# Second batch of a routed-FFN kernel: its ScalarE, VectorE and TensorE work dealt out anew, and a fifth staging place for expert weights

## What is computed

```python
# attention-like mixer, per batch of 512 tokens
sim = einsum(Q, K) / (sqrt(32) * 4)            # 512 x 512, Q and K from ctx
threshold = top_k(sim, 153)[0][:, :, -1:]      # the 153rd largest of each row
A = sigmoid(sim) * (sim >= threshold)
A = (A + swapaxes(A, -1, -2)) * 0.5
x = x + (1 - g) * layernorm(x) + g * A         # g = sigmoid(gamma_raw)
# feed-forward on xn = layernorm(x), 2048 tokens, 8 experts, 2 for each token
shared = silu(xn @ s_gate_w + s_gate_b) * (xn @ s_up_w + s_up_b) @ s_down_w + s_down_b
moe = sum over experts of weight * (silu(xn @ gate) * (xn @ up)) @ down
out = x + moe + shared
```

## Time and profile before

| what | value |
|---|---|
| median of 3 runs | 521.26 us |
| profiled execution, its own time | 522.16 us |
| its span, first to last instruction | 520.3 us |
| TensorE busy | 457.6 us, 88% of the span |
| VectorE busy | 335.3 us, 64% |
| ScalarE busy | 254.1 us, 49% |
| GpSimd busy | 149.0 us, 29% |
| mean granted TensorE clock | 0.946 |
| chain that ended last | TensorE 73%, VectorE 14%, ScalarE 4% |

### The profile page before, as it was taken

One profiled execution on the slowest core, in us unless ns is written; L12 is line 12 of the kernel. 1 busy time (PEld: TensorE's weight loads), 2 busy tenths in 40 slices (PEclk: granted clock), 3 DMA queues, 4 the chain that ended last, 5 costly groups with the idle time before them and its releaser, 6 DMA issues.

```text
span 520.3 us, 9112 instructions
## 1 busy us (share of the span) xinstructions
PE 457.6 (88%) x2619; PEld 257.8 (50%) x2620; DVE 335.3 (64%) x959; ACT 254.1 (49%) x469; POOL 149.0 (29%) x199
## 2 busy tenths in 40 slices
PE   7406775999999999899997999999999999999960
PEld 3204332545454545354444666666666666666630
DVE  4879799799999999737956555555556433333310
ACT  5884546347934792335543455555545333333320
POOL 2010100013001300220042554555545444444431
PEclk9755996999999999999998999999999999999995
DMA  8801520028302800285368888778777545545541
GB/s 277 240 1 69 179 96 2 0 81 195 70 1 82 146 18 1 94 151 110 90 164 213 189 201 190 189 174 199 182 185 171 87 84 85 86 82 88 90 69 22
DMA packets 39005, 60.53 MB, mean 116 GB/s; under 512 B 8233, under 2 KB 18729, under 8 KB 38962
## 3 DMA queue, kind: packets, MB, share of 16 engines
q0 software_dynamic: 10384, 23.38, 26.9%
q1 hardware_dynamic: 26514, 36.61, 22.5%
q10 hardware_dynamic: 2064, 0.02, 0.2%
HBM read 37.68 MB, written 22.30 MB: 115 GB/s over the span
## 4 chain that ended last, share of the span: by engine, by line
PE 73%; DVE 14%; ACT 4%; issue 3%; DMA 2%; POOL 1%; SPq 0%; DVEq 0%; POOLq 0%; ACTq 0%
PE bank L988 5%; PE bank L990 5%; PE bank L989 5%; PE bank L1156 4%; PE bank L1155 4%; PE bank L1154 4%; PE bank L1130 4%; PE bank L1132 4%; PE bank L1131 4%; PE bank L1133 4%; PE bank L1134 4%; PE bank L1135 4%; PE bank L1000 3%; PE bank L1114 3%; PE bank L935 3%
## 5 line engine op out<-in xcount | busy, mean ns | idle before, releaser
L547 POOL DMA_INDIRECT out_dram<-xb,sidx x35 | 55.9, 1597 | 85.2 <-ACT xb L850 73.5
L988 PE MATMUL bank<-xT,W 128*128 128x512 f16 x176 | 67.9, 386 | 8.5 <-DVE sgt L1491 8.5
L989 PE MATMUL bank<-xT,W 128*128 128x512 f16 x176 | 67.7, 385 | 0.0
L990 PE MATMUL bank<-xT,W 128*128 128x512 f16 x176 | 67.7, 385 | 0.0
L1623 DVE TENSOR_TENSOR hS<-bank,hS 128x384 f16<-128x384 f32 x35 | 19.5, 557 | 69.6 <-ACT hS L842 69.6
L836 ACT ACTIVATE sgt<-bank 128x352 f32<-128x352 f32 x35 | 16.2, 464 | 70.6 <-PE bank L1135 70.6
L850 ACT ACTIVATE xb<-bank,wcol 128x512 f32<-128x512 f32 x35 | 24.0, 687 | 53.4 <-PE bank L1156 53.4
L1130 PE MATMUL bank<-W,xT 128*128 x140 | 44.1, 315 | 1.1 <-DVE W L1215 1.0
L1132 PE MATMUL bank<-W,xT 128*128 x140 | 44.1, 315 | 0.0
L1131 PE MATMUL bank<-W,xT 128*128 x140 | 44.1, 315 | 0.0
L1133 PE MATMUL bank<-W,xT 128*128 x140 | 44.1, 315 | 0.0
(11 more groups left out here) (254 smaller groups left out, 1037.3 us busy)
## 6 DMA issues: line engine op xcount, KB each, us to landing
out_dram<-W POOLq DMA_DIRECT2D x12, 256.0 KB, 5.1
stage<-L_ffn_down_w_in SPq DMA_DIRECT2D x12, 256.0 KB, 4.1
sim<-L_ffn_down_w_in SPq DMA_DIRECT2D x12, 256.0 KB, 3.8
stage<-L_ffn_gate_w_in SPq DMA_DIRECT2D x16, 176.0 KB, 3.4
stage<-L_ffn_up_w_in SPq DMA_DIRECT2D x16, 176.0 KB, 4.5
sim<-L_ffn_gate_w_in SPq DMA_DIRECT2D x16, 176.0 KB, 3.7
sim<-L_ffn_up_w_in SPq DMA_DIRECT2D x16, 176.0 KB, 4.7
W<-x_in SPq DMA_DIRECT2D x2, 1024.0 KB, 6.5
```

The costliest lines, as they stand in the source:

```text
L988: pe.matmul(o, wh, xT[:, 0, c, :], start=(c == 0), stop=False)
L989: pe.matmul(o, wh, xT[:, 1, c, :], start=False, stop=False)
L990: last = pe.matmul(o, wl, xT[:, 0, c, :], start=False, stop=(c == KD - 1))
```

## The change

Each part of it, by the names above:

- **Counting.** In batch 1 (the second) ScalarE counts three tiles and VectorE one (`act_tiles`); the other batches keep two and two. `target` has a row for each case.
- **ScalarE's order in batch 1** is written out (`second_batch`): Silu 0 ahead of the count of probe 1, Silu 1 ahead of probe 3, the sigmoids after probe 3 and Silu 2. That takes three table loads where there was one.
- **VectorE's order in batch 1**: `shared_hidden(0, 0)` in probe 1 and `shared_hidden(0, 1)` in probe 3 (before: in probe 3 and after it); the logits are copied in probe 0 and their eight largest are found in batch 2 for eight tiles at once; the statistics of tiles 2 and 3 of the new scores are taken ahead of `x_lo`.
- **x of batch 1** is loaded right after the first inputs, and its sums are taken by ScalarE (`x_total`, `x_mean` in the first batch, `x_square` before the first count) instead of bn_stats on VectorE.
- **End of batch 0 on ScalarE**: context copy, four roundings and projection copy come ahead of `apply_ln(0)`.
- **End of batch 0 on TensorE**: seven matmuls on zeros after the projection (`keep_on`), then for tiles 0 and 1 the masked matrix itself goes into the bank (`masked_A`) and the transpose is added to it, as an ordinary matmul with the identity; VectorE leaves out two of the four L1422.
- **Staging**: five places, the fifth behind the two over the scores; the pace is SECOND_AT = [2, 2, 0, 0] and BLOCK_AT = [2, 3, 3, 2, ...].

```diff
-ACT_TILES = 2
+MAX_ACT_TILES = 3
...
-PLACES = 4
+PLACES = 5
...
+def act_tiles(b):
+    return MAX_ACT_TILES if b == 1 else 2
...
-SECOND_AT = [2, 2, 2, 0]
-BLOCK_UNITS = 2
+SECOND_AT = [2, 2, 0, 0]
+BLOCK_AT = [2, 3, 3] + [2] * (HEAD_BLOCKS - 3)
...
-    sim = sb("sim", [P, TB, S])
+    simf = sb("simf", [P, (PLACES - 2) * SI])[:, :]
+    sim = simf[:, 0:TB * S].rearrange("p (a b) -> p a b", a=TB)
...
+        load_x(1)
         for b in range(NB):
...
-            if b == 0:
-                load_x(1)
...
             for t in range(TB):
                 sig_scores(0, t)
+            context_T(1)
+            split_some(SC - 2)
+            proj(1)
             apply_ln(0)
-            context_T(1)
-            split_some(SC)
-            proj(1)
-            for f in range(LOW_PARTS):
+            split_some(2)
+            for f in range(4):
                 round_low(f)
+            for t in range(TB):
+                x_total(1, t)
+            x_mean(1)
+            for f in range(4, LOW_PARTS):
+                round_low(f)
...
+        def second_batch():
+            sh_sig(0, 0)
+            count(1, 1)
+            count(1, 2)
+            sh_hi(0, 0)
+            sh_sig(0, 1)
+            count(1, 3)
+            context_T(2)
+            sh_hi(0, 1)
+            sh_sig(0, 2)
+            for t in range(TB):
+                sig_scores(1, t)
+            proj(2)
+            sh_hi(0, 2)
+            sh_sig(0, 3)
+            apply_ln(1)
...
             if b == 0:
+                for t in range(TB):
+                    x_square(1, t)
                 count(1, 0)
...
+        def masked_A(t):
+            if t == 0:
+                pe.wait_ge(s_rw, 1)
+            pe.wait_ge(s_A, t + 1)
+            pe.matmul(bank[AT_BANK[t]][:, :], ident[:, :], sim[:, t, :], start=True, stop=False)
...
+                keep_on(7, bank[3])
+                for t in range(SUMMED):
+                    masked_A(t)
...
+            if b == 1 and it == 0:
+                x_variance(1)
+                copy_logits(0)
+            if b == 1 and it == 1:
+                shared_hidden(0, 0)
+            if b == 1 and it == 2:
+                layer_norm_x(1)
+                weight_lo(12)
+            if b == 1 and it == 3:
+                shared_hidden(0, 1)
+                weight_lo(13)
...
-            for t in range(TB):
+            for t in range(0 if b else SUMMED, TB):
                 last = dve.scalar_tensor_tensor(xs[b % 2][:, t, :], sim[:, t, :], gam[:, 3:4], xs[b % 2][:, t, :], ALU.mult, ALU.add)
```

More of the change, by code:

```diff
@@ L99, with counts_before @@
 LAST = LATE + PER_EXPERT
+def act_tiles(b):
+    return MAX_ACT_TILES if b == 1 else 2
+def counts_before(b):
+    return PROBES * sum(act_tiles(i) for i in range(b))
+SUMMED = 2
+X_STEPS = 2 * TB + 1
 PE_LOWS = range(KD, 2 * KD)
@@ L486, in _ @@
         pool.memset(pw[:, 1, :], -0.5)
-        pool.memset(target[:, 0:TB - ACT_TILES], MIDDLE)
-        pool.memset(target[:, TB - ACT_TILES:TB], 2 * MIDDLE - S).then_inc(s_const, 1)
+        for b in range(2):
+            dve_tiles = TB - act_tiles(b)
+            pool.memset(target[:, b, 0:dve_tiles], MIDDLE)
+            last = pool.memset(target[:, b, dve_tiles:TB], 2 * MIDDLE - S)
+        last.then_inc(s_const, 1)
         pool.wait_ge(s_const, 4)
@@ L879, in _, with keep_on @@
     def _(pe):
-        def keep_on(n):
+        def keep_on(n, o=bank[7]):
             for _ in range(n):
-                pe.matmul(bank[7][:, :], zeros16[:, 0:P], zeros16[:, 0:512], start=True, stop=True)
+                pe.matmul(o[:, :], zeros16[:, 0:P], zeros16[:, 0:512], start=True, stop=True)
         def form_low(f):
@@ L948, in transpose_A @@
             for m in range(TB):
-                last = pe.transpose(bank[AT_BANK[t]][:, m * P:(m + 1) * P], sim[:, m, t * P:(t + 1) * P], ident[:, :])
-            last.then_inc(s_AT, 1)
+                o, a = bank[AT_BANK[t]][:, m * P:(m + 1) * P], sim[:, m, t * P:(t + 1) * P]
+                if b == 0 and t < SUMMED:
+                    last = pe.matmul(o, a, ident[:, :], start=False, stop=(m == TB - 1))
+                else:
+                    last = pe.transpose(o, a, ident[:, :])
+            last.then_inc(s_AT, 1)
+        def masked_A(t):
[3 more added lines that the diff above has]
+            pe.matmul(bank[AT_BANK[t]][:, :], ident[:, :], sim[:, t, :], start=True, stop=False)
         def transpose_xn(b, t):
@@ L1337, in threshold_end @@
             link(last)
-            if b:
+            if b > 1:
                 shared_hidden(b - 1, 1)
@@ L1467, in largest_logits @@
             dve.wait_ge(s_lgc, b + 1)
-            for g in range(TB * b, TB * (b + 1)):
+        def largest_logits(tiles):
+            for g in tiles:
                 last = dve.max(mx[:, g, :], lg[:, g, :])
             link(last)
-            for g in range(TB * b, TB * (b + 1)):
+            for g in tiles:
                 last = dve.max_index(mxi[:, g, :], mx[:, g, :], lg[:, g, :])
```

133 lines of the change are left out of this document (73 added, 60 removed).

## The result

The changed kernel took 516.89 us in the median of 5 runs (515.21 to 517.92), the kernel before 521.81 beside it (520.79 to 523.19): a ratio of 0.9888, 95% interval 0.9857 to 0.992. It is faster, by 4.9 us. The forecast was 512.8 with 515.9 as the upper end: right in sign, 4.1 us too low, and outside the range. The profiled execution took 515.21 us, span 513.4; TensorE busy 461.2 us (90%), VectorE 327.9 (64%), ScalarE 264.4 (51%), GpSimd 151.0 (29%); mean granted clock 0.959.

What follows compares the result with a forecast made beforehand. TensorE was taken as the bound from batch 1's start on, with one large hole in batch 1. Terms -8.8 + 0.3 + 0 = -8.5 us, taken from a median of 521.26, gave 512.8 us, range 509.8 to 515.9.

Steps and rivals of the forecast that it cites:

- The hole of batch 1: TensorE's wait before chunk 2 of the shared up product: 8.5 us of idle and 2.7 of low clock vanish.
- The new waits: TensorE in batch 1 would newly idle 1.2 us before chunk 4 and 2.4 before the transposes, 3.6 together.
- The end of batch 0: Earlier mask and fewer VectorE additions start batch 1 1.2 us earlier; bounds from a 0.7 loss to a 2.7 gain.
- I take a clock that rises midway: At batch 0's end TensorE would leave the transposes at about 49 us with the high clock reached.
- Batch 2: Finding the largest logits of eight tiles instead of four on VectorE costs 0.3 us, between 0 and 1.05.
- Staging: Fifth place and new pace of splits, felt in the routed blocks: 0 us, between -1 and +1.
- Profile to median: Whole kernel: the median was taken 0.90 us below the profiled execution, as in the kernel before.
- 1, a drain beside each table load: Each table switch stalls ScalarE 1.28 us more, 1.0 us in all: 513.8 us, chance 0.08.
- 2, a clock that falls again before the transposes: Batch 1's mask comes one or two us later and TensorE's clock may fall: 515.5 us, chance 0.12.
- 3, the better clock: Clock stays high over batch 0's end and at the routed blocks' start, 1.5 us each: 509.8 us, chance 0.10.
- 4, late gathers: Weight transfers one unit further ahead delay gathers in the routed blocks, 1 us per block: 532.8 us, chance 0.04.
- 5, a hole that only moves: Silu 0 stays late and batch 1's hole moves from chunk 2 to chunk 4: about 520.5 us, chance 0.04.

Runs made afterwards that it cites:

- g5: The kernel before with 38 zero matmuls filling TensorE's hole in batch 1; 519.86 us, 0.9963 of the kernel before.
- f2: The changed kernel with 30 zero matmuls ahead of batch 0's second projection and 20 instead of 7 behind it; 512.99 us, 0.9846 of the kernel before.
- e4: The changed kernel repeated unchanged in a later group of runs; 515.12 us, 0.988 of the kernel before.
- h3: The changed kernel repeated word for word in another later group; 514.79 us, 0.9868 of the kernel before.
- i1: The changed kernel with block 0's split put back ahead of the shared output on ScalarE, new pace and five places kept; 515.52 us, 0.9867 of the kernel before.
- g3: g2 plus unread matmuls at the start of the routed blocks, nine in the first and four in the second; 511.94 us, 0.9811 of the kernel before.
- h1: g3 plus 6, 4 and 6 zero matmuls in the three idle times of batch 0's last steps; 509.48 us, 0.9773 of the kernel before.
- g4: The kernel before with 46 zero matmuls ahead of batch 0's second projection and 18 behind it; 521.59 us, 0.9997 of the kernel before.
- i3: h1 repeated word for word in a later group; 510.43 us, 0.9778 of the kernel before.
- f1: The changed kernel with SUMMED = 0, so no masked matrix goes through TensorE; 516.68 us, 0.9897 of the kernel before.
- h2: g3 repeated word for word beside h1; 511.08 us, 0.9783 of the kernel before.
- g2: f2 with the old pace of staging, five places kept; 513.92 us, 0.985 of the kernel before.

## Why the prediction was right and wrong

- **The hole of batch 1: right.** Chunk 2 follows the transposes without idle time; Silu 0 went at 68.62 (forecast 67.9), and g5 prices the low clock at 2.74 us (2.7).
- **The new waits: right in place, a little smaller than forecast.** Before chunk 4 1.09 us (forecast 1.2), before the transposes 1.85 (2.4), both ended by VectorE.
- **The end of batch 0: mis-sized.** The mask came at 41.54 (41.3), but "I take a clock that rises midway" did not hold: it was low to about 48 us, TensorE left the transposes at 49.47 and not at about 49, and the start of batch 1 gained 62.96 - 62.42 = 0.54 us, not 1.2. The bounds were nearly right: with fillers (f2), the gain to the router matmuls is 2.97 us against an upper end of 2.7. No row stood beside the forecast's 1.75 us for a masked matrix and 0.43 for an ordinary transpose; the two masked matrices took 45.98 - 42.44 = 3.54 us, 1.77 each. In e4 and h3 the gain is 1.11 and 1.84, and a low stretch of 1.7 us behind it takes that back.
- **Batch 2:** from transposes to transposes 0.22 us more than before (forecast 0.3). That the larger search of logits is the cause was argued; no run took it out.
- **Staging: the first failed step.** "Nothing gained and nothing lost: 0" costed the splits by the busy shares of ScalarE and VectorE in the routed blocks. It left out the diff's exchange of split and shared output. ScalarE's splits of block 0 now wait 3.21 us for TensorE's down product, VectorE's halves wait 3.79 for them and stand ahead of its hidden product, and TensorE waits 1.02. From the first routed matmul to the last pass 229.18 us, before 227.61: +1.57, where the forecast was 0 and the slow end +1. Of this, 1.40 are the two steps that i1 put back. An average of free time says nothing of two steps that change places.
- **Profile to median: the other failed step.** "The median of before lies 0.90 lower, so the forecast for the median is 521.26 - 8.5" carried the offset of one profiled execution of before over to the changed kernel. That took 2.58 us off: the changed kernel's profile was its fastest of five executions. In later groups its median was 515.12 and 514.79, which the range would have held, so part of this miss is the draw of the first five executions. Part is the place of the low stretches. The mean clock is on record for each of the 15 executions: the three near 517.9 us have 0.955 to 0.958, the others 0.958 to 0.966. No profile of the changed kernel near 517.9 exists. The nearest is i1's, at 518.37 us: against the first profile it loses 2.64 us at batch 1's start and 1.94 up to the routed blocks, both beside a low stretch, and gains 1.40 in the routed blocks by its own edit. These sum to 3.18, and its span is 3.1 us longer. That the slow executions of the changed kernel are of this kind is likely by that, not shown. Neither failed step alone would have carried the time out of the range; 1.57 and 2.58 us together did.
- **The rivals.** 1, a drain beside each table load, fell: loads at 80.63 and 87.59 are followed at 81.92 and 88.89, after 1.28 us and with no idle entry. By the Trainium skill (ScalarE: Activation LUTs, section What ACT_TABLE_LOAD costs) a further 1.38 us should lie there; the rows do not have it. 2, a clock that falls again before the transposes, did not happen after the new waits; it happened ahead of chunk 0 in other executions, and its price was 1.7 to 2.6. 3, the better clock, did not come by itself, but it names the two places where fillers then helped: with both filled g3 reached 511.94, and h1, with batch 1's start filled too, 509.48, where the rival said 509.8. 4, late gathers: TensorE waited for no gather in the routed blocks. 5, a hole that only moves: no.

## What to carry to other kernels

Write out where TensorE's stream is thin but not empty, and put the clock that each execution might get there into the range: here 1.3 to 2.6 us a stretch. Take the offset between a profiled execution and the median from several executions, or widen the range by it. Matmuls without a reader were a cure here where the length of the wait was known, and gained nothing where they ended early and then ran at the low clock (g4). The fastest version here, h1 and i3, is 0.9773 and 0.9778 of the kernel before; the change alone is 0.9868 to 0.9888. And cost every pair of steps that a diff exchanges, also where it looks like housekeeping.

## What was not expected of the hardware

The granted clock fell although no single idle time of TensorE was longer than 1.39 us in the 16 us before (h3: waits of 1.39 and 0.87 us ending at 55.75 and 57.98, low from 58 to 66; a third, of 1.41, came in the low stretch). It fell also at 213 to 217 us, behind a wait of 2.0 us at batch 3's L1018, in f1, h2 and i1 and not in the changed kernel's profile, which has the same wait. The program alone does not fix where it falls: the changed kernel's three profiles show three patterns. And with the same 30 zero matmuls ahead, f2 was low from 35 to 39 us, behind a wait of 2.56 us, while g2, behind one of 1.73, stayed at 1.00 from 28 to 50 us.
